# First attention of a two-layer block: output and query projections issued in halves, key and value projections one step later

## The reference, cut to what matters

```
qkv = x @ W_qkv + b_qkv
q, k, v = (qkv[:, :, 0], qkv[:, :, 1], qkv[:, :, 2])
k = k + pos_enc[None, :, None, :]
scores = jnp.einsum('bqhd,bkhd->bhqk', q, k) / scale
attn = jax.nn.softmax(scores, axis=-1)
out = jnp.einsum('bhqk,bkhd->bqhd', attn, v).reshape(b, s, H * D)
return out @ W_out + b_out
```

## Time and profile before

| | us |
|---|---|
| median of 3 runs | 2145.54 |
| lowest and highest of them | 2140.77, 2154.2 |
| profiled execution, its own time | 2144.52 |
| span of the profiled execution | 2142.7 |
| granted TensorE clock, mean | 0.971 |

### The profile page before, as it was taken

One profiled execution on the slowest core, in us unless ns is written; L12 is line 12 of the kernel. 1 busy time (PEld: TensorE's weight loads), 2 busy tenths in 40 slices (PEclk: granted clock), 3 DMA queues, 4 the chain that ended last, 5 costly groups with the idle time before them and its releaser, 6 DMA issues.

```text
span 2142.7 us, 35861 instructions
## 1 busy us (share of the span) xinstructions
PE 2060.6 (96%) x12074; PEld 945.5 (44%) x12074; DVE 1692.1 (79%) x2739; ACT 1702.3 (79%) x2299; POOL 1284.4 (60%) x777
## 2 busy tenths in 40 slices
PE   6999999999999999999999989999999999999996
PEld 2544445445444445454454433333333433443445
DVE  7677787877877878777887837789999999999903
ACT  1678888888888888888888984388878878888883
POOL 1588898897997987988988795333032024016003
PEclk7899999999999999999999998599999999999998
DMA  3000000000000000000000100000000000000000
GB/s 105 20 16 20 27 16 31 16 17 30 16 28 19 16 31 16 27 20 16 31 16 27 40 16 20 1 1 2 2 1 1 2 2 7 1 2 6 1 2 11
DMA packets 32039, 36.33 MB, mean 17 GB/s; under 512 B 12340, under 2 KB 23228, under 8 KB 31736
## 3 DMA queue, kind: packets, MB, share of 16 engines
q1 hardware_dynamic: 31864, 34.03, 5.1%
HBM read 32.46 MB, written 1.43 MB: 16 GB/s over the span
## 4 chain that ended last, share of the span: by engine, by line
PE 80%; ACT 7%; DVE 6%; issue 3%; POOL 3%; DMA 0%; DVEq 0%; ACTq 0%; POOLq 0%
PE acc_o L538 18%; PE scores L516 14%; PE acc_o L658 11%; PE scores L644 10%; PE ring L491 8%; ACT prob L846 3%; DVE mxp L1521 3%; PE ring L624 2%; POOL accp L1016 2%; PE ring L708 2%; PE ring L717 2%; ACT prob L868 2%; PE ring L468 2%; ACT scores L853 2%; PE ring L456 2%
## 5 line engine op out<-in xcount | busy, mean ns | idle before, releaser
L1404 DVE TENSOR_REDUCE mxp<-ring 128x1 f32<-128x512 f32 x1024 | 656.3, 685 | 231.3 <-PE ring L491 214.6
L1016 POOL TENSOR_TENSOR accp<-accp,prob 128x1024 f32<-128x1024 f32 x318 | 799.8, 2515 | 54.5 <-ACT prob L846 11.0
L868 ACT ACTIVATE prob<-scores 128x512 f32<-128x512 f32 x1024 | 545.3, 601 | 135.6 <-PE scores L644 132.9
L846 ACT ACTIVATE prob<-scores 128x1024 f32<-128x1024 f32 x512 | 520.0, 1016 | 147.1 <-PE scores L516 127.9
L516 PE MATMUL scores<-q_all,k_all 64*128 64x512 f32 x3072 | 545.4, 409 | 7.2 <-ACT scores L853 4.9
L1521 DVE TENSOR_REDUCE mxp<-ring 128x1 f32<-128x512 f32 x789 | 510.7, 684 | 52.4 <-PE ring L624 39.9
L853 ACT ACTIVATE scores<-minus_all 128x1024 f32<-128x1024 f32 x510 | 525.2, 1030 | 24.2 <-ACT prob L846 0.8
L538 PE MATMUL acc_o<-prob,v 128*64 128x512 f32 x2048 | 500.3, 609 | 2.9 <-ACT v L828 2.9
L491 PE MATMUL ring<-k_all,q_all 64*128 64x512 f32 x1024 | 392.8, 432 | 10.1 <-DVE mxp L1404 5.5
L516 PEld LDWEIGHTS scores<-q_all,k_all 64*128 64x128 f32 x3072 | 336.2, 186 | 84.8 <-ACT scores L853 41.2
L644 PE MATMUL scores<-q_all,k_all 32*128 32x512 f32 x1024 | 308.1, 494 | 12.7 <-ACT prob L868 8.5
(11 more groups left out here) (197 smaller groups left out, 1553.9 us busy)
## 6 DMA issues: line engine op xcount, KB each, us to landing
minus_all<-m_dram SPq DMA_DIRECT2D x32, 512.0 KB, 3.6
rec<-rec_dram SPq DMA_DIRECT2D x60, 128.0 KB, 2.8
w_all<-w_pairs SPq DMA_DIRECT2D x1, 1344.0 KB, 11.2
x<-x SPq DMA_DIRECT2D x4, 256.0 KB, 3.8
pos_sb<-pos SPq DMA_DIRECT2D x1, 1024.0 KB, 7.6
w_all<-w SPq DMA_DIRECT2D x1, 1024.0 KB, 5.6
minus_all<-w SPq DMA_DIRECT2D x4, 256.0 KB, 3.6
q_all<-m_rows SPq DMA_DIRECT2D x64, 2.0 KB
```

The costliest lines, as they stand in the source:

```text
L846: nc.scalar.activation(prob[:, T % SLOTS1, :, :], sc[T % 2][:, :, :], ACT.Exp, scale=SCALE1).then_inc(exp_done, 1)
L868: nc.scalar.activation(prob2[:, h // 2, T % 2, h % 2, :], sc2[place % 3], ACT.Exp, scale=SCALE2).then_inc(exp2_done, 1)
L1016: nc.gpsimd.tensor_tensor(accp[:, k % 2], accp[:, k % 2], prob[:, T % SLOTS1], ALU.add).then_inc(pool_acc, 1)
L1404: done(nc.vector.reduce_max(mxp1[k % 2][:, h * QT + q, kc:kc + 1], bank[:], AX.X), ("max", k, q, kc, h))
```

## The change

`y(k)` for chunks 0 to 27 is issued as two items of two quarters each: "ya" at step 7 of chunk k + 1, "y" at step 0 of chunk k + 2. The queries' projection of chunks 4 to 31 is issued as two items of 256 columns each: "Qa" at step 4 and "Q" at step 6 of chunk k - 3. The key or value projection that stood at step 0 stands at step 1. Every half takes a ring bank of its own on PE and on DVE: two more uses of the ring for each chunk. The split of the keys that stood behind POOL's third add stands behind its fifth. The order of the other work stays.

```diff
+HALVED_Y = range(CHUNKS1 - NC)
+HALVED_Q = range(NC, CHUNKS1)
...
     if j == 4 and k + 3 < CHUNKS1:
+        return ("Qa" if k + 3 in HALVED_Q else "Q", k + 3)
+    if j == 6 and k + 3 in HALVED_Q:
         return ("Q", k + 3)
     if j == (2 if k < LAST1 else 1) and k > 0:
         return ("sums", k - 1)
-    if j in (0, 5) and k // NC + 1 < PAIRS:
-        half = 0 if j == 0 else 1
+    if j == 0 and k - 2 in HALVED_Y:
+        return ("y", k - 2)
+    if j in (1, 5) and k // NC + 1 < PAIRS:
+        half = 0 if j == 1 else 1
         return ("K", k // NC + 1, 2 * c + half) if c < 2 else ("V", k // NC + 1, 2 * (c - 2) + half)
     if j == 3 and k + 1 < CHUNKS1:
         return ("fin", k + 1)
     if j == (7 if k < LAST1 else 4) and k > 0:
-        return ("y", k - 1)
+        return ("ya" if k - 1 in HALVED_Y else "y", k - 1)
...
+        def quarters_y(k, part):
+
+            if k not in HALVED_Y:
+                return range(QT)
+            return range(QT // 2) if part == "ya" else range(QT // 2, QT)
+
+        def cols_q(k, part):
+
+            if k not in HALVED_Q:
+                return 0, CW
+            return (0, CW // 2) if part == "Qa" else (CW // 2, CW)
+
+        def q_written(k, part="Q"):
+
+            return k + 1 + max(k - NC, 0) + (part == "Q" and k in HALVED_Q)
...
+            def q_proj(k, part="Q"):
                 p, c = k // NC, k % NC
-                bank = begin(("Q", k))
-                end(nc.tensor.matmul(bank[:], w_all[:, p, 0:128], xnt[:, c * CW:(c + 1) * CW], start=True, stop=True),
-                    ("Q", k))
+                bank = begin((part, k))
+                first, end_ = cols_q(k, part)
+                end(nc.tensor.matmul(bank[:, first:end_], w_all[:, p, 0:128], xnt[:, c * CW + first:c * CW + end_],
+                                     start=True, stop=True), (part, k))
...
-                pe.wait_ge(qh_ready, k + 1)
+                pe.wait_ge(qh_ready, q_written(k))
...
                     wait_free(pe, ("Q", k))
+                    if k in HALVED_Q:
+                        wait_free(pe, ("Qa", k))
...
+            def y(k, part="y"):
+                bank = begin((part, k))
+                for q in quarters_y(k, part):
                     pe.wait_ge(onorm_ready, k + 1 if k < LAST1 else k + 1 + q)
                     last = nc.tensor.matmul(bank[:, q * 128:(q + 1) * 128], onorm[:, q * 128:(q + 1) * 128],
                                             wout_sb[:, k // NC, :], start=True, stop=True)
-                end(last, ("y", k))
+                end(last, (part, k))
...
-                    if t == 3 and last_item1(k, 0) and last_item1(k, 0)[0] == "K":
-                        split_keys(*last_item1(k, 0)[1:])
+                    if t == 5 and k > 0 and last_item1(k, 1) and last_item1(k, 1)[0] == "K":
+                        split_keys(*last_item1(k, 1)[1:])
...
+            def q_proj(k, part="Q"):
                 p, c = k // NC, k % NC
-                bank = open_(("Q", k))
+                bank = open_((part, k))
                 bias = bqk_all[:, p, 0:1]
-                nc.vector.tensor_scalar(qhi[:, c, :], bank[:], bias, None, ALU.add).then_inc(qh_ready, 1)
-                dve.wait_ge(qh_ready, k + 1)
-                done(nc.vector.scalar_tensor_tensor(qlo[:, c, :], bank[:], bias, qhi[:, c, :].bitcast(F32),
-                                                    ALU.add, ALU.subtract), ("Q", k))
+                cols = slice(*cols_q(k, part))
+                nc.vector.tensor_scalar(qhi[:, c, cols], bank[:, cols], bias, None, ALU.add).then_inc(qh_ready, 1)
+                dve.wait_ge(qh_ready, q_written(k, part))
+                done(nc.vector.scalar_tensor_tensor(qlo[:, c, cols], bank[:, cols], bias, qhi[:, c, cols].bitcast(F32),
+                                                    ALU.add, ALU.subtract), (part, k))
...
+            def y(k, part="y"):
                 c = k % NC
-                bank = open_(("y", k))
+                bank = open_((part, k))
                 if k >= NC:
-                    wait_free(dve, ("y", k - NC))
+                    wait_free(dve, (part, k - NC))
+                    if k not in HALVED_Y:
+                        wait_free(dve, ("ya", k - NC))
                 else:
                     dve.wait_ge(row_ready, 1)
-                done(nc.vector.tensor_tensor(x1[:, c * QT:(c + 1) * QT, :], x1[:, c * QT:(c + 1) * QT, :],
-                                             bank[:].rearrange("p (t n) -> p t n", t=QT), ALU.add), ("y", k))
+                tiles = quarters_y(k, part)
+                rows = x1[:, c * QT + tiles[0]:c * QT + tiles[-1] + 1, :]
+                done(nc.vector.tensor_tensor(rows, rows, bank[:, tiles[0] * 128:(tiles[-1] + 1) * 128]
+                                             .rearrange("p (t n) -> p t n", n=DM), ALU.add), (part, k))
```

More of the change, by code:

```diff
@@ L451, in tokens1 @@
                 end(last, ("T", c))
-            def q_proj(k):
+            def q_proj(k, part="Q"):
                 p, c = k // NC, k % NC
-                bank = begin(("Q", k))
-                end(nc.tensor.matmul(bank[:], w_all[:, p, 0:128], xnt[:, c * CW:(c + 1) * CW], start=True, stop=True),
-                    ("Q", k))
+                bank = begin((part, k))
+                first, end_ = cols_q(k, part)
+                end(nc.tensor.matmul(bank[:, first:end_], w_all[:, p, 0:128], xnt[:, c * CW + first:c * CW + end_],
+                                     start=True, stop=True), (part, k))
             def k_proj(p, b):
@@ L551, in sums @@
                 end(last, ("sums", k))
-            def y(k):
-                bank = begin(("y", k))
-                for q in range(QT):
+            def y(k, part="y"):
+                bank = begin((part, k))
+                for q in quarters_y(k, part):
                     pe.wait_ge(onorm_ready, k + 1 if k < LAST1 else k + 1 + q)
@@ L564, in item1 @@
                     tokens1(it[1])
-                elif kind == "Q":
-                    q_proj(it[1])
+                elif kind in ("Q", "Qa"):
+                    q_proj(it[1], kind)
                 elif kind == "K":
@@ L579, in item1 @@
                     sums(it[1])
+                elif kind == "ya":
+                    y(it[1], "ya")
                 else:
@@ L1453, in reciprocals @@
                 nc.vector.reciprocal(rec[:, cols], ssum[:, cols]).then_inc(rec_ready, 1)
-            def y(k):
+            def y(k, part="y"):
                 c = k % NC
-                bank = open_(("y", k))
+                bank = open_((part, k))
                 if k >= NC:
-                    wait_free(dve, ("y", k - NC))
+                    wait_free(dve, (part, k - NC))
+                    if k not in HALVED_Y:
+                        wait_free(dve, ("ya", k - NC))
                 else:
                     dve.wait_ge(row_ready, 1)
-                done(nc.vector.tensor_tensor(x1[:, c * QT:(c + 1) * QT, :], x1[:, c * QT:(c + 1) * QT, :],
-                                             bank[:].rearrange("p (t n) -> p t n", t=QT), ALU.add), ("y", k))
+                tiles = quarters_y(k, part)
+                rows = x1[:, c * QT + tiles[0]:c * QT + tiles[-1] + 1, :]
+                done(nc.vector.tensor_tensor(rows, rows, bank[:, tiles[0] * 128:(tiles[-1] + 1) * 128]
+                                             .rearrange("p (t n) -> p t n", n=DM), ALU.add), (part, k))
             def item1(it):
                 kind = it[0]
-                if kind == "Q":
-                    q_proj(it[1])
+                if kind in ("Q", "Qa"):
+                    q_proj(it[1], kind)
                 elif kind == "K":
@@ L1476, in item1 @@
                     fin(it[1])
-                elif kind == "y":
-                    y(it[1])
+                elif kind in ("y", "ya"):
+                    y(it[1], kind)
             link(nc.vector.memset(ones64[:], 1.0))
```

## The result

The changed kernel takes 2157.49 us (median of 8 runs, 2152.41 to 2163.75) against 2145.55 us for the kernel before (8 runs, 2140.77 to 2154.2). The ratio is 1.0059, with a 95% interval from 1.0042 to 1.0076: a small loss, clear of noise. The profiled execution took 2157.01 us, its span is 2155.2 us, 12.5 us longer than before. Lines moved with the edit: 491 is now 517 (max tiles), 516 is 544 (scores), 538 is 566 (values), 557 is 585 (y), 456 is 482 (queries), 461 is 487 (keys); on VectorE (DVE) 1404 is 1435, 1440 is 1471, 1398 is 1429, 1462 is 1497, 1388 is 1419; on GpSimd (POOL) 1013 is 1043, 1016 is 1046, 1002 and 1004 are 1032 and 1034.

What follows compares the result with a forecast made beforehand. The prediction took TensorE's chain as the bound. Thirteen keys chunks (+11.4 us), fourteen values chunks (-1.3) and chunks 28 and 29 (about 0.5 gained) made +9.6 on 2144.5, so 2154 us, range 2122 to 2176.

Steps and rivals of the forecast that it cites:

- The stalls that go: PE's waits for ScalarE's seed in steps 7 and 2, up to 0.6 us each, vanish; step 4's stall stays.
- The late item of step 1: Step 1's key or value item waits for DVE's second max tile, starts at 2.79; the step lasts 5.7 us.
- d = 1.44: Time in us from step 1's start until DVE reads its first max tile; up to 0.69 does no harm.
- The 5.85 us between the ends of adds 13 and 14: DVE's add waits for POOL's, so this interval stays 5.85 us whatever DVE does between.
- ScalarE's lag after the copy of acc_o: ScalarE's 0.6 us copy delays step 0's first exponential, adding 0.25 us of lag to step 1's 5.2.
- Step 2: Keys chunks: 5.6 us, sums 0.7 late; values chunks: 4.91, DVE's add 15 first by 0.07 us.
- Step 7 of keys chunks: If DVE's add 12 meets POOL's second key split, the step is 0.85 us longer; half, 0.4, was taken.
- The sum: Keys chunks 39.25 us (+0.88), values chunks 38.26 (-0.09), about 0.5 gained in chunks 28 and 29; together +9.6.
- A: Rival: DVE's lateness is absorbed, 27 chunks x -0.65 - 0.5 = -18, 2127 us; chance 0.22.
- A2: Rival: all stalls vanish and halves cost nothing, 27 x -1.4 = -38, 2107 us; chance 0.03.
- B: Rival: pile-up in keys chunks once DVE is 1.7 us late in step 7, 13 x 2 = 26, 2180 us; chance 0.18.
- C: Rival: half operations cost as much as whole ones, PE +1.3 us a chunk, 2165 to 2185; chance 0.05.

Runs made afterwards that it cites:

- e1: Kernel before with only the queries' projection halved, y whole at step 7, keys or values at step 0: 2135.36 us, ratio 0.9954.
- e3: Changed kernel with POOL's adds 2 and 4 of each chunk but the last cut to 8 columns, sums incomplete: 2124.75 us, ratio 0.9900 to the kernel before.
- e7: Changed kernel with the items of steps 0 and 1 exchanged, key split behind POOL's third add: 2149.04 us, ratio 1.0024 to the kernel before.
- e5: Changed kernel with DVE's adds 13, 14 and 15 moved behind their step's second max tile: 2134.06 us, ratio 0.9952 to the kernel before.
- e6: As e5, with DVE's add 12 also moved ahead of the half query item: 2138.33 us, ratio 0.9969 to the kernel before.
- e2: Kernel before with only y halved and keys or values at step 1, queries' projection whole at step 4: 2156.33 us, ratio 1.0057.

## Why the prediction was right, step by step

The forecast of 2154 us was 3.5 us low. The mechanism was the one that it gave; one term was too small, and a gain that it did not have hid part of that (below).

**The stalls that go.** Step 7 of values chunks lasts 4.57 us (4.50 forecast), step 2 4.86 (4.91), steps 4 4.68 to 4.83 (4.83). e1 shows the part in steps 4 and 6 alone.

**The late item of step 1.** Forecast 5.7 us at d = 1.44, measured 5.52 at d = 1.26. The 5.85 us between the ends of adds 13 and 14 held exactly; what was off is the length of steps 7 and 0, 9.16 us together instead of 9.00, since half a y costs about 0.64 us on PE (738.94 to 739.58 in step 0 of chunk 17) and not 0.58. A longer step takes up lateness. e3 takes the wait away and the step falls to 4.97, so the cause is shown, not only argued. The 5.2 us that I gave this step without the lock was itself 0.2 too long: 4.97 is a bare step and the item, so ScalarE's lag after the copy of acc_o costs nearly nothing there.

**Step 2.** In values chunks DVE won the race for add 15, as forecast; e7 shows the same race lost. In keys chunks forecast 5.6, measured 5.72.

**Step 7 of keys chunks is the term that I mis-sized.** I gave 0.4 for "half of it", since the order of add 12 and the second split operation was within my uncertainty. The price of one meeting (0.85) was right, 5.36 us against 4.55; but it happens in 11 of the 12 steady keys chunks, not in half of them. Only chunk 16 escapes, with 4.61: POOL was later there, and DVE issued add 12 at 731.75, 0.06 us before the second split operation at 731.81 (both rows stand first in the timelines above); the split then took 2.32 us instead of 1.29. Schedules repeat from chunk to chunk, and so do their races; a chance of one half should have been a choice of 0 or 0.85.

**The sum.** Keys chunks 39.74 us (39.25 forecast), values chunks 38.24 (38.26). For the span: 11 keys chunks x 1.39 and chunk 16 with 0.6 are +15.9, values chunks -1.0, chunks 28 and 29 -0.4, chunks 30 and 31 +0.7, chunk 2 -0.5. Chunk 1 gives back 2.4, with its clock at 1.00 where it was 0.96 (the windows above); I had forecast no gain there. Together 12.3 of the 12.5; a start 0.8 us longer and an end 0.5 shorter make up the rest. The steady keys chunks alone stand 5.3 us above the forecast (12 x 0.88 = 10.6), and chunk 1, which it had at +0.9, hides 3.3 of that. That the total is only 3 us off is in part luck.

**Rivals.** A is out: DVE's lateness was not absorbed. The steps became shorter, but the 5.85 us from add 13 to add 14 did not, and the first tile of step 1 was read at d = 1.26. A2 is out too: step 4 of keys chunks, with half a query item, lasts 4.83 us, as forecast with its stall kept. B did not come: d in step 7 stayed at 1.53, under the edge of 1.7, and add 13, issued at 775.49, was still ahead of POOL's at 775.65, by 0.16 us. That it was so near is why the range had to be wide. C is out, since half a y costs PE 0.64 us where the whole cost 1.08. But halves are dearer than half. On DVE they take 475 and 410 ns for 751 and 688 before (both above the prediction's estimate of 0.39 us for 256 columns). On PE two halves of y in steps of their own cost 0.2 us more than the whole, and so do the two of the queries: in e1 step 4 loses 0.42 us and step 6 gains 0.62. That is 0.4 us a chunk, some 11 us in 27 chunks, where the forecast had 0.3. The stalls that went pay for it: values chunks come out 0.1 us shorter.

## What to carry to other kernels

An engine's idle time says little about whether it can take an item: what counts is how late it is at the place where the item needs it, and a step without an item may be the very thing that hides this. Where two engines exclude each other, follow one constant interval (here 5.85 us from add to add) through the new order, and ask at each meeting who issues first. Before spreading work over more steps, try moving the operation that waits behind the reads that others need; it changed 23 us here (e5 against the changed kernel), where halving the queries' projection gained 10 (e1).

## What the runs showed of the hardware

The lock held for whole operations, in both directions. DVE's add of two SBUF tiles waited for POOL's adds, and for the key splits, and POOL's add waited for DVE's (3.30 us at 775.65, where 2.4 is usual), while DVE's operations with a bank as source ran beside them without loss (0.75 us at 745.27). The Trainium skill, page "SBUF — State Buffer", section "SBUF: two separate sides", states just that; e3 and e5 put a price on it.

One thing I had not expected: step 7 of chunk 1 varied from 5.85 us (changed kernel) to 10.3 (e6) between the complete kernels. Where it took 8.7 to 10.3 us, DVE had first waited 1.7 to 3.2 us for POOL's last add, PE had stood idle for 2.1 to 3.9 us behind it, and the granted clock of the chunk was 0.94 to 0.97, that is, a piece of it at the lower level of 1.2 GHz. Where it took 5.9 to 6.9 (changed kernel, e2, e5), the clock was 1.00. A change in the steady part of this kernel can gain or lose 4 us in this one place.
